# Self-attention of the second layer: the statistics of a coming batch from slot 4 to slot 7, its normalisation from slot 6 to slot 3 of the next batch

## The chip, the cores and the metric

The kernel runs on one core of one Trainium2 chip. Its engines run side by side and meet only at semaphores: PE (TensorE, matmuls), DVE (VectorE), ACT (ScalarE), POOL (GpSimd) and SP, which here only issues transfers. The metric is the device time of one execution in microseconds (us), lower is better, as the median of several runs.

## What is computed

The whole network is two gated layers of attention and feed-forward over x of shape (16, 256, 128). The change touches one of its eight phases, the causal self-attention of the second layer: 16 batches of 256 tokens with 128 channels, 16 heads of width 32. `_ln` at its head is the part that is moved.

```python
def _ln(x, g, b):
    m = jnp.mean(x, -1, keepdims=True)
    v = jnp.var(x, -1, keepdims=True)
    return (x - m) * jax.lax.rsqrt(v + 1e-05) * g + b

def _mha(x, y, ...):                       # here y is x
    xn = _ln(x, lnx_g, lnx_b)
    yn = _ln(y, lny_g, lny_b)
    q = jnp.einsum('bsc,hcd->bhsd', xn, wq)
    k = jnp.einsum('btc,hcd->bhtd', yn, wk)
    v = jnp.einsum('btc,hcd->bhtd', yn, wv)
    a = jax.nn.softmax(jnp.einsum('bhsd,bhtd->bhst', q, k) * D ** (-0.5), axis=-1)
    mask = (jnp.arange(t)[None, :] > jnp.arange(s)[:, None])
    a = a * mask
    o = jnp.einsum('bhst,bhtd->bhsd', a, v)
    x_out = x + o @ li1_w + li1_b
```

## The kernel before, in words

`network` lists eight phases, and between two phases all engines meet. The phase of the change is `SelfAttention(k, "d", 32, "after", ...)`, and in it `a.G` is 4. Phase "a", the first layer's self-attention, uses the same code with `a.G` 1 and other slots.

Each engine has a program of its own that walks the same slots, eight to a batch (`a.per`). A slot i of batch b is one unit, four heads by 128 queries by 256 keys. I number the slots of a batch 0 to 7. The order within an engine is fixed by this code; nothing is scheduled at run time.

In each slot PE runs a **window**: the scores of unit i (L441), then the transposed scores of unit i - 6 (`a.lag`) with their maxima subtracted (L466, L470). A window of slot i + 1 waits until the maxima and the exponentials of slot i are done, since both lie in the same PSUM banks (`wait(pe, s["maxed"], 2 * ...)` and `wait(pe, s["exped"], 2 * t)`). While DVE takes the maxima (L697, two per slot) and ACT the exponentials (L611, two per slot), PE runs `values` of unit i - 8 (L520, L525, L532) and then the slot's pieces.

The pieces and steps are in the table `SLOTS[4]`. Letters: T transposes the normalised input on PE (L547) and DVE scales it out of PSUM (L759, L760); Q, V are projections (PE L414, ACT L633, L634, L647); N transposes the split maxima (PE L576, then DVE L771); Y is the output projection (PE L414, DVE L778); U, R, M are steps on DVE alone (L729, L738, L745). The ones that matter here:

- slot 1: N of the second half of the batch in front, then V
- slot 3: R (a DVE transpose of 128x512, L738) and V
- slot 4: T of the next batch, M (a DVE multiplication of two SBUF tensors, L745), Q
- slot 5: N and Y; slot 7: `save_denominators` (L719) and Y

POOL masks each unit after its exponentials (L843), adds the two units of a pair in every odd slot (L851, 128x1024), splits the maxima of each half batch into bf16 parts (`split`, L822 to L830) at the head of slots 0 and 4, and adds a bias (L810) in slot 5.

The normalisation of batch b + 2 runs ahead of its use in three parts. `norm_stats` on DVE: two bn_stats (L166) and two bn_aggr (L171). `rstd` on POOL: an addition (L219) and a power (L221), behind a wait on `aggr`. `norm` on DVE: two tensor_scalar of 128x128 from SBUF to SBUF (L193), behind a wait on `rstd`. Before, DVE does the statistics at the end of slot 4 of batch b and `norm` at the end of slot 6; POOL does `rstd` at the end of slot 4. Piece T in slot 4 of batch b + 1 reads the result. Batches 0 and 1 are normalised ahead of the phase, so 14 batches go through this code.

SP loads x of batch b + 2 once `norm` of batch b has released the buffer (`wait(sp, s["wn"], b - 1)` in `sync_self`, called with b + 2). Behind it in SP's queue stand the load of the residual input, which waits for POOL's bias of an earlier batch, some transfers of blanks, and a store.

Of the kernel before, what the change touches and what calls it, by code (L numbers as in the profile page):

```python
# [6 lines left out]
B, S, C = 16, 256, 128  # L7
# [34 lines left out]
class Count:  # L42


    def __init__(self, sem):
        self.sem, self.n = sem, 0
# [194 lines left out]
class SelfAttention:  # L241
# [21 lines left out]
    def __init__(self, k, name, D, mask, src, base, dst, ctx, w):  # L263
        self.k, self.name, self.D, self.mask = k, name, D, mask
        self.src, self.base, self.dst, self.ctx, self.ctx_norm, self.w = src, base, dst, ctx, False, w
        self.scale = float(D) ** -0.5
        self.G = H * D // P
        self.units, self.lag = self.UNITS[self.G], {1: 8, 4: 6}[self.G]
        self.per = len(self.units)
        self.first_max = [0, 4]  # L270
        self.nv, self.ends, self.nq = (1, 1, 2) if self.G == 1 else (2, 2, 4)
        self.weights_ahead, self.loaded_ahead, self.ahead_over = [], None, 4
        each = dict(x_in=16, base_in=16, stored=16, stats=1, aggr=1, eps_in=1, rstd=1, wn=1, t_full=1, side=1, q_full=self.G,
                    q_ready=self.nq, v_full=self.nv, v_ready=self.nv, window=self.per, maxed=2 * self.per, exped=2 * self.per,
                    split=10, turned_max=2, max_ready=2, masked=8, pv_done=self.per, num_saved=QUADS if self.G == 4 else 1,
                    den_saved=1, rden=1, r_full=self.ends, ot=self.ends, y_full=self.ends, res=self.ends, biased=1)
        if self.G == 1:
            each.update(k_full=1, km_ready=QUADS + 1, ctx_in=16)
        if mask == "after":
            each.update(summed=QUADS)  # L280
        self.s = k.signals(each, B)
        sem, n = k.counts["window"]
        k.counts["window"] = sem, n + self.lag
# [81 lines left out]
def wait(eng, signal, n):  # L365

    if n > 0:
        eng.wait_ge(signal.sem, signal.base + n)
# [308 lines left out]
def vector_self(dve, a):  # L677
# [4 lines left out]
    def maxima(i):  # L682

        b, c, e = a.unit(i)
        t, part = i - a.lag, a.part(i)
        wait(dve, s["window"], i + 1)
        wait(dve, s["split"], 5 * (part - 1))
        for pair in range(2):
            if pair == 1 and a.is_unit(t):
                wait(dve, s["exped"], 2 * t + 1)  # L690
            out, banks = k.nmax[:, part % 2, 6 * e:6 * e + 6], a.score_banks(pair)
            if c == a.CROSS:
                last = dve.tensor_reduce(out[:, 2:6, 2 * pair:2 * pair + 2].rearrange("p c j -> p j c"),
                                         banks[:, :, 0:S].rearrange("p n (c t) -> p n c t", c=4), AX.X, ALU.max, negate=True)
            else:
                n = (e + 1) * P if a.mask == "before" else S
                last = dve.tensor_reduce(out[:, c % 2, 2 * pair:2 * pair + 2], banks[:, :, 0:n], AX.X, ALU.max, negate=True)  # L697
            last.then_inc(s["maxed"].sem, 1)

    def own_values(bank, b, blk):  # L700

        return dve.tensor_tensor(
            k.val[:, b % 2, blk].rearrange("p (r j c) -> p r j c", r=4, c=32),
            bank[:, blk * P:(blk + 1) * P].rearrange("p (r c) -> p r c", r=4).unsqueeze(2).to_broadcast([P, 4, 4, 32]),
            k.own_columns[:, :, :].unsqueeze(1).to_broadcast([P, 4, 4, 32]), ALU.mult)
# [8 lines left out]
    def save_denominators(b):  # L714

        wait(dve, s["pv_done"], a.per * (b + 1))
        wait(dve, s["rden"], b)
        if a.G == 4:
            dve.transpose(k.den[:, 0:S], k.turned[0][:, b % 2 * S:(b % 2 + 1) * S]).then_inc(s["den_saved"].sem, 1)  # L719
        else:  # L720
            dve.transpose(k.den, k.turned[0][:, :]).then_inc(s["den_saved"].sem, 1)
# [59 lines left out]
    for i in a.slots:  # L781
        if a.is_unit(i):
            maxima(i)
        n = i - a.lag - LATER
        if a.is_unit(n) and n % a.per == a.per - 1:
            save_denominators(n // a.per)
        for kind, m, b, which in a.pieces(i):
            piece(kind, m, b, which)
        for kind, m, b in a.steps(i):
            step(kind, m, b)  # L790
        for kind, m, b, which in a.pieces(i - 1):
            if kind == a.V and a.G == 1:
                own_values(a.bank(which), b, 1)
                cross_values(a.bank(which), b).then_inc(s["v_ready"].sem, 1)
        ahead = i // a.per + 2
        if 2 <= ahead < B and i % a.per == 4:
            norm_stats(Step(ahead))
        if 2 <= ahead < B and i % a.per == 6:
            norm(Step(ahead))


def gpsimd_self(pool, a):
    k, s, w = a.k, a.s, a.w

    rstd = attention_rstd(pool, a)

    def bias(b):
        wait(pool, s["base_in"], 16 * (b + 1))
        wait(pool, s["res"], a.ends * (b - 1))
        pool.tensor_tensor(k.base_sum[:, b % 2], k.base_in[:, b % 2], w["o_bias"].unsqueeze(1).to_broadcast([P, SB, C]), ALU.add)\  # L810
            .then_inc(s["biased"].sem, 1)

    def split(part):

        wait(pool, s["maxed"], 2 * a.part_end(part))
        wait(pool, s["turned_max"], part - 1)
        heads = 6 if a.G == 1 and part % 2 else 2
        order = lambda x: x.rearrange("p (e c) j -> p e j c", e=2)[:, :, :, 0:heads]
        parts = [k.nmax3[:, part % 2].rearrange("p e (j x) -> p e j x", x=32)[:, :, :, n:n + 3 * heads - 2:3] for n in range(3)]
        whole, rest = order(k.nmax[:, part % 2]), [order(k.nrest[:, n]) for n in range(2)]  # L820
        done = 5 * part
        pool.tensor_copy(parts[0], whole).then_inc(s["split"].sem, 1)  # L822
        wait(pool, s["split"], done + 1)
        pool.tensor_tensor(rest[0], whole, parts[0], ALU.subtract).then_inc(s["split"].sem, 1)
        wait(pool, s["split"], done + 2)
        pool.tensor_copy(parts[1], rest[0]).then_inc(s["split"].sem, 1)
        wait(pool, s["split"], done + 3)
        pool.tensor_tensor(rest[1], rest[0], parts[1], ALU.subtract).then_inc(s["split"].sem, 1)
        wait(pool, s["split"], done + 4)
        pool.tensor_copy(parts[2], rest[1]).then_inc(s["split"].sem, 1)  # L830

    def mask(t):

        b, c, e = a.unit(t)
        wait(pool, s["exped"], 2 * (t + 1))
        blk = a.keys_block(e)
        block = k.pt[:, t % TURNED, :, blk * P:(blk + 1) * P]
        if a.mask == "before":
            pool.affine_select(out=block, in_=block, compare_op=ALU.is_ge, fill=0.0, base=0, pattern=[[0, 4], [1, P]],  # L839
                               channel_multiplier=-1).then_inc(s["masked"].sem, 1)  # L840
        else:
            wait(pool, s["pv_done"], t - TURNED + 1)
            pool.affine_select(out=k.pm[:, t % TURNED], in_=block, compare_op=ALU.is_ge, fill=0.0, base=-1, pattern=[[0, 4], [-1, P]],  # L843
                               channel_multiplier=1).then_inc(s["masked"].sem, 1)

    def add(t):

        b, c, e = a.unit(t)
        wait(pool, s["exped"], 2 * (t + 1))
        wait(pool, s["pv_done"], t - 3)  # L850
        pool.tensor_tensor(k.both[:, c % 2], k.pt[:, (t - 1) % TURNED], k.pt[:, t % TURNED], ALU.add).then_inc(s["summed"].sem, 1)  # L851

    for i in a.slots:
        for part in range(2 * B):
            if a.part_end(part) == i:
                split(part)
        if a.is_unit(i - a.lag) and a.unit(i - a.lag)[1] < a.CROSS:
            mask(i - a.lag)
            if a.mask == "after" and (i - a.lag) % 2 == 1:
                add(i - a.lag)  # L860
        ahead = i // a.per + 2
        if 2 <= ahead < B and i % a.per == 4:
            rstd(Step(ahead))
        if i % a.per == 5 and 0 <= i // a.per - 1 < B:
            bias(i // a.per - 1)
# [1773 lines left out]
```

## Time and profile before

| | |
|---|---|
| time, median of 3 runs | 1555.57 us (1554.34 to 1556.86) |
| the profiled execution | 1551.26 us |
| its span in the profile | 1549.5 us |
| PE busy | 1322.5 us (85%) |
| DVE busy | 927.1 us (60%) |
| POOL busy | 769.1 us (50%) |
| ACT busy | 705.7 us (46%) |

The phase of the change runs from about 601 to 990 us of the span. A busy share over the whole span says little about one phase, so the rows below are taken from the order of time within one batch (window of slot 2 at 684.96 us to window of slot 2 at 708.74 us, a period of 23.78 us), from the summaries of waits, and from two places where engines met one another. In the views in order of time a row gives the start, the time from the first start to the last end of what is merged in it, engine, line, operation, what is written and read, and how many instructions; in brackets stands the idle time of the engine just before, and who ended it.

### The profile page before, as it was taken

The numbers are of one execution on the slowest core, as the hardware profiler recorded it, in microseconds if no ns is written. First come the engines' busy times: TensorE is split into PE (matmuls) and PEld (weight loads), VectorE is DVE, ScalarE is ACT, GpSimd is POOL, SyncE is SP. The second block draws the span as 40 slices with busy tenths as digits, with TensorE's granted clock in tenths as the row PEclk, the third lists the DMA queues.
The fourth block names the chain that finished last, engine by engine and source line by source line (L and its number), as shares of the span: only waits on it lengthen the run. The fifth ranks groups of instructions, "written<-read, shape, count | busy, mean of one in ns | idle before, by whom it ended". The sixth has DMA issues, their size and how long they took to land. (4 is left out here: it accounts for less than half of the span.)

```text
span 1549.5 us, 56395 instructions
## 1 busy us (share of the span) xinstructions
PE 1322.5 (85%) x22833; PEld 843.6 (54%) x22834; DVE 927.1 (60%) x2397; ACT 705.7 (46%) x1485; POOL 769.1 (50%) x1355
## 2 busy tenths in 40 slices
PE   3899999999985977999999999596999996893786
PEld 2555555555544653555555555364555554572676
DVE  3566666767654555776767766355467766584343
ACT  1455555455543434555565666242244442430443
POOL 3233333323330673877778787577222222576355
PEclk8899999999997888999999999798599999896899
DMA  3340000000000135334243342121011101232221
GB/s 80 78 131 18 21 17 21 14 21 13 14 9 22 55 102 156 105 93 132 68 133 103 98 126 68 42 82 56 20 32 36 34 24 47 86 103 73 68 77 49
DMA packets 145313, 97.92 MB, mean 63 GB/s; under 512 B 20533, under 2 KB 141964, under 8 KB 145068
## 3 DMA queue, kind: packets, MB, share of 16 engines
q1 hardware_dynamic: 142252, 88.06, 20.7%
q0 software_dynamic: 2816, 6.37, 1.1%
q8 instruction: 181, 2.97, 0.8%
q14 instruction: 64, 0.52, 0.1%
HBM read 40.31 MB, written 54.61 MB: 61 GB/s over the span
## 5 line engine op out<-in xcount | busy, mean ns | idle before, releaser
L611 ACT ACTIVATE space<-scores 128x512 f32<-128x512 f32 x576 | 314.0, 551 | 334.4 <-PE scores L470 221.1
L697 DVE TENSOR_REDUCE space<-scores 128x2 f32<-128x512 f32 (+1 forms) x512 | 306.7, 622 | 213.4 <-PE scores L470 147.5
L839 POOL TENSOR_SCALAR_AFFINE_SELECT space<-space 128x512 f32<-128x512 f32 x128 | 81.3, 635 | 274.0 <-ACT space L611 274.0
L441 PE MATMUL scores<-space 32*128 32x256 f32 (+1 forms) x2304 | 193.7, 404 | 22.8 <-DVE space L697 16.6
L470 PE MATMUL scores<-space 32*128 32x256 f32 (+1 forms) x2048 | 151.0, 357 | 1.5 <-issue 1.5
L851 POOL TENSOR_TENSOR space<-space 128x1024 f32<-128x1024 f32 x64 | 151.3, 2364 | 0.0
L441 PEld LDWEIGHTS scores<-space 32*128 32x128 f32 x2304 | 95.0, 188 | 88.4 <-DVE space L697 77.0
L843 POOL TENSOR_SCALAR_AFFINE_SELECT space<-space 128x512 f32<-128x512 f32 x128 | 88.0, 687 | 72.6 <-ACT space L611 72.5
L470 PEld LDWEIGHTS scores<-space 32*128 32x128 f32 x2048 | 84.5, 187 | 19.0 <-issue 2.1
L466 PE MATMUL scores<-space,selectors 32*128 32x256 bf16 (+1 forms) x1024 | 73.2, 255 | 6.5 <-issue 5.0
L166 DVE BATCH_NORM_STATS2 space<-space 128x6 f32<-128x128 f32 (+1 forms) x304 | 67.0, 273 | 18.2 <-DMA space<-xo 16.9
L1097 ACT ACTIVATE space<-scores 128x512 f32<-128x512 f32 x64 | 37.9, 597 | 82.4 <-PE scores L1006 77.7
L437 PE MATMUL scores<-above_parts,ident_parts 32*128 32x128 bf16 (+3 forms) x2048 | 42.8, 200 | 32.3 <-DVE space L697 20.4
L511 PE MATMUL turned<-space,ones_column 128*32 128x128 f32 (+1 forms) x1024 | 68.9, 341 | 0.3 <-POOL space L839 0.3
L437 PEld LDWEIGHTS scores<-above_parts,ident_parts 32*128 32x128 bf16 x2048 | 30.1, 94 | 70.6 <-DVE space L697 50.4
L1414 PE MATMUL turned<-w_a_li_w,space 128*128 128x128 f32 x512 | 67.3, 285 | 1.1
L1468 ACT ACTIVATE space<-scores,w_later_cols 128x512 f32<-128x512 f32 x96 | 59.4, 676 | 19.2 <-PE scores L1401 18.8
L1480 ACT ACTIVATE space<-space 128x128 f32<-128x128 f32 x72 | 29.7, 482 | 83.7 <-POOL space L1682 83.7
L514 PE MATMUL num<-space 128*32 128x128 f32 (+1 forms) x1024 | 65.5, 328 | 0.0
L1152 DVE TENSOR_REDUCE space<-scores 128x8 f32<-128x512 f32 x64 | 42.2, 692 | 38.2 <-PE scores L1006 33.2
L1414 PEld LDWEIGHTS turned<-w_a_li_w,space 128*128 128x128 f32 x512 | 61.6, 196 | 6.2 <-ACT space L1468 4.1
L1401 PE MATMUL scores<-space,w_a_li_w 128*128 128x512 f32 x128 | 62.9, 638 | 1.9 <-DVE space L1519 1.9
(324 smaller groups left out, 2877.6 us busy)
## 6 DMA issues: line engine op xcount, KB each, us to landing
by_expert<-blank SPq DMA_DIRECT2D x33, 1040.0 KB, 9.5
space<-by_expert SPq DMA_DIRECT2D x40, 130.0 KB
space<-in_x SPq DMA_DIRECT2D x32, 128.0 KB, 2.2
space<-xx SPq DMA_DIRECT2D x32, 128.0 KB, 2.5
xo<-space SPq DMA_DIRECT2D x32, 128.0 KB, 2.6
space<-xo SPq DMA_DIRECT2D x16, 256.0 KB
space<-xm SPq DMA_DIRECT2D x32, 128.0 KB, 2.2
w_w<-in_L_ffn_w SPq DMA_DIRECT2D x8, 256.0 KB
```

The lines of the kernel that those rows point to most:

```text
L166: last = dve.bn_stats(stats[:, blk], x[:, blk])
L437: pe.matmul(a.score_bank(j)[:, e * P + 32 * part:n], k.ident_parts[rows, part], k.above_parts[rows, part, 32 * part:P], start=(part == 0), ...
L441: last = pe.matmul(a.score_bank(j)[:, 0:n], q[rows, e * P:(e + 1) * P], keys[rows, 0:n], start=not cut, stop=True, skip_group_check=True)
L466: pe.matmul(a.score_bank(j)[:, S + lo:2 * S], k.selectors[rows, c % 2], a.maxima(t)[rows, lo:S], start=True, stop=False, skip_group_check= ...
L470: last = pe.matmul(a.score_bank(j)[:, S + lo:2 * S], keys[rows, blk * P:(blk + 1) * P], q[rows, lo:S], start=False, stop=True, skip_group_ ...
L511: pe.matmul(strip(k.turned[0], j)[:, lo:S], k.ones_column[:, c], pt[:, j, lo:S], start=first, stop=done, skip_group_check=True)
L611: act.activation(pt[:, 2 * pair:2 * pair + 2, lo:S], a.score_banks(pair)[:, :, S + lo:2 * S], ACT.Exp, bias=0.0, scale=1.0)\
L697: last = dve.tensor_reduce(out[:, c % 2, 2 * pair:2 * pair + 2], banks[:, :, 0:n], AX.X, ALU.max, negate=True)
L839: pool.affine_select(out=block, in_=block, compare_op=ALU.is_ge, fill=0.0, base=0, pattern=[[0, 4], [1, P]], channel_multiplier=-1).then_i ...
L843: pool.affine_select(out=k.pm[:, t % TURNED], in_=block, compare_op=ALU.is_ge, fill=0.0, base=-1, pattern=[[0, 4], [-1, P]], channel_multi ...
L851: pool.tensor_tensor(k.both[:, c % 2], k.pt[:, (t - 1) % TURNED], k.pt[:, t % TURNED], ALU.add).then_inc(s["summed"].sem, 1)
L1414: last = pe.matmul(k.turned[t.parity][:, blk * P:(blk + 1) * P], k.mh[:, t.parity, f, blk * P:(blk + 1) * P], w["w2"][:, f], start=(f == 0 ...
```

## The change

It gives the two slots names, `stats_slot` and `norm_slot`. For `a.G` 1 they keep their values (4 and 6). For `a.G` 4 the statistics go to slot 7, on DVE and with `rstd` on POOL, and `norm` goes to slot 3 of the next batch. The distance in batches is counted anew there, so that the same batches are normalised, one slot ahead of piece T that reads them.

```diff
+        self.stats_slot, self.norm_slot = {1: (4, 6), 4: (7, 3)}[self.G]
...
         ahead = i // a.per + 2
-        if 2 <= ahead < B and i % a.per == 4:
+        if 2 <= ahead < B and i % a.per == a.stats_slot:
             norm_stats(Step(ahead))
-        if 2 <= ahead < B and i % a.per == 6:
+        if a.norm_slot < a.stats_slot:
+            ahead = i // a.per + 1
+        if 2 <= ahead < B and i % a.per == a.norm_slot:
             norm(Step(ahead))
...
         ahead = i // a.per + 2
-        if 2 <= ahead < B and i % a.per == 4:
+        if 2 <= ahead < B and i % a.per == a.stats_slot:
             rstd(Step(ahead))
```

DVE, from the end of slot 2 to slot 6 of a batch in the middle of the phase, before. `space` is the name under which all SBUF work tiles go:

```order
L745 TENSOR_TENSOR space<-space 128x512
L697 TENSOR_REDUCE space<-scores 128x2 x2
L738 STREAM_TRANSPOSE space<-space 128x512
L697 TENSOR_REDUCE space<-scores 128x2 x2
L759 TENSOR_SCALAR space<-misc,w_later_cols 128x256
L760 TENSOR_SCALAR space<-misc,w_later_cols 128x256
L745 TENSOR_TENSOR space<-space 128x512
L166 BN_STATS space<-space 128x6 x2
L171 BN_AGGR space<-space 128x2 x2
L697 TENSOR_REDUCE space<-scores 128x2 x2
L771 COPY space<-turned 128x256
L778 TENSOR_TENSOR space<-misc,space 128x128
```

The same place now, with the line numbers of the changed file (one more for these lines):

```order
L746 TENSOR_TENSOR space<-space 128x512
L698 TENSOR_REDUCE space<-scores 128x2 x2
L739 STREAM_TRANSPOSE space<-space 128x512
L193 TENSOR_SCALAR space<-space 128x128 x2
L698 TENSOR_REDUCE space<-scores 128x2 x2
L760 TENSOR_SCALAR space<-misc,w_later_cols 128x256
L761 TENSOR_SCALAR space<-misc,w_later_cols 128x256
L746 TENSOR_TENSOR space<-space 128x512
L698 TENSOR_REDUCE space<-scores 128x2 x2
L772 COPY space<-turned 128x256
L779 TENSOR_TENSOR space<-misc,space 128x128
```

The four instructions of the statistics are gone from between M of slot 4 and the maxima of slot 5, and the two of `norm` stand between R of slot 3 and the maxima of slot 4.

POOL, from the mask of slot 4 over the bias to the split at the head of the next batch's slot 0, before:

```order
L843 AFFINE_SELECT space<-space 128x512
L219 TENSOR_TENSOR space<-space,eps 128x2
L221 TENSOR_TENSOR space<-space,minus_half 128x2
L843 AFFINE_SELECT space<-space 128x512
L851 TENSOR_TENSOR space<-space 128x1024
L810 TENSOR_TENSOR space<-space,w_a_li_b 128x256
L843 AFFINE_SELECT space<-space 128x512 x2
L851 TENSOR_TENSOR space<-space 128x1024
L822 CAST nmax<-space 128x8x2
```

The same place now, where the line numbers of POOL's program are higher by three:

```order
L846 AFFINE_SELECT space<-space 128x512 x2
L854 TENSOR_TENSOR space<-space 128x1024
L813 TENSOR_TENSOR space<-space,w_a_li_b 128x256
L846 AFFINE_SELECT space<-space 128x512 x2
L854 TENSOR_TENSOR space<-space 128x1024
L219 TENSOR_TENSOR space<-space,eps 128x2
L221 TENSOR_TENSOR space<-space,minus_half 128x2
L825 CAST nmax<-space 128x8x2
```

The two instructions of `rstd` have moved from between two masks to between the addition of slot 7 and the split of slot 0.

## Rows read from the trace of the kernel before

**Rows 1.** Busy time in the stretch 601 to 986 us; then PEclk, DMA share, GB/s.

```profile
601.00:986.00 385.00, 362.59 (x6810) 212.88 (x6810) 260.44 (x510) 226.29 (x470) 297.81 (x389) 1.00 0.35 96
```

**Rows 2.** Waits of PE, 660 to 935 us: total us, times, longest.

```profile
PE scores L441 <- DVE space L697: 4.6, 11, 0.4
```

**Rows 3.** DVE in order of time, slots 3 to 7 and the next slot 0.

```profile
690.26 0.70 DVE L738 STREAM_TRANSPOSE space<-space 128x512 f32<-128x512 f32 x1
691.86 1.32 DVE L697 TENSOR_REDUCE space<-scores 128x2 f32<-128x512 f32 x2 [0.91 <-PE scores L470]
693.64 0.54 DVE L759 TENSOR_SCALAR space<-misc,w_later_cols 128x256 f32<-128x256 f32 x1 [0.46 <-PE misc L547]
...
694.56 0.68 DVE L745 TENSOR_TENSOR space<-space 128x512 f32<-128x512 f32 x1
695.15 0.48 DVE L166 BATCH_NORM_STATS2 space<-space 128x6 f32<-128x128 f32 x2
...
695.83 1.25 DVE L697 TENSOR_REDUCE space<-scores 128x2 f32<-128x512 f32 x2
...
699.77 1.17 DVE L193 TENSOR_SCALAR space<-space 128x128 f32<-128x128 f32 x2
...
704.13 1.32 DVE L697 TENSOR_REDUCE space<-scores 128x2 f32<-128x512 f32 x2 [0.90 <-PE scores L470]
```

**Rows 4.** PE in order of time, same batch: windows of slots 5, 6, and N.

```profile
693.53 0.71 PE L441 MATMUL scores<-space 32*128 32x256 f32 x8
...
694.18 0.61 PE L470 MATMUL scores<-space 32*128 32x256 f32 x8
...
695.73 1.08 PE L414 MATMUL misc<-w_a_li_w,space 128*32 128x128 f32 x32
697.22 0.71 PE L441 MATMUL scores<-space 32*128 32x256 f32 x8 [0.42 <-DVE space L697]
...
707.53 0.29 PE L576 MATMUL turned<-identb,nmax 128*128 128x128 bf16 x2
```

**Rows 5.** POOL in order of time, same batch.

```profile
690.41 0.64 POOL L843 TENSOR_SCALAR_AFFINE_SELECT space<-space 128x512 f32<-128x512 f32 x1 [1.71 <-ACT space L611]
691.01 2.37 POOL L851 TENSOR_TENSOR space<-space 128x1024 f32<-128x1024 f32 x1
...
695.25 0.63 POOL L843 TENSOR_SCALAR_AFFINE_SELECT space<-space 128x512 f32<-128x512 f32 x1
696.00 0.19 POOL L219 TENSOR_TENSOR space<-space,eps 128x2 f32<-128x2 f32 x1
696.27 0.70 POOL L221 TENSOR_TENSOR space<-space,minus_half 128x2 f32<-128x2 f32 x1
...
697.81 2.37 POOL L851 TENSOR_TENSOR space<-space 128x1024 f32<-128x1024 f32 x1
700.13 0.73 POOL L810 TENSOR_TENSOR space<-space,w_a_li_b 128x256 f32<-128x256 f32 x1
...
703.27 2.37 POOL L851 TENSOR_TENSOR space<-space 128x1024 f32<-128x1024 f32 x1
705.58 0.23 POOL L822 CAST nmax<-space 128x16 bf16<-128x16 f32 x1
...
706.79 0.22 POOL L830 CAST nmax<-space 128x16 bf16<-128x16 f32 x1
```

**Rows 6.** POOL and PE in order of time, where PE waited for a split.

```profile
970.24 0.22 POOL L830 CAST nmax<-space 128x16 bf16<-128x16 f32 x1
...
970.61 0.27 PE L576 MATMUL turned<-identb,nmax 128*128 128x128 bf16 x2 [0.73 <-POOL nmax L830]
```

**Rows 7.** POOL and DVE in order of time, where M met an addition.

```profile
971.58 2.35 POOL L851 TENSOR_TENSOR space<-space 128x1024 f32<-128x1024 f32 x1
971.86 2.62 DVE L745 TENSOR_TENSOR space<-space 128x512 f32<-128x512 f32 x1
```

**Rows 8.** All of line 193: duration in ns, least, median, most.

```profile
L193 DVE TENSOR_SCALAR space<-space x96: 245/342/766, 18.9 to 1259.0; 128x128 f32<-128x128 f32 x96
```

## The prediction

> **What bounds the kernel now.** I read the page's list of busy times first, then the phase alone. From 601 to 986 us PE is busy for 362.6 of 385 us at a granted clock of 1.00, the upper level, 2.4 GHz [rows 1]. So PE sets the pace here, and an edit on DVE or POOL counts only by what it adds to or takes from PE's idle time. Next I read the summary of PE's waits: between 660 and 935 us it waits 11 times for DVE's maxima at the head of a window, 4.6 us in all, 0.42 us each [rows 2]. That is once a batch (a batch takes about 24 us), and the order of time shows where: the window of slot 6, at 697.22, starts 0.42 us after PE has run out of work [rows 4]. Its cause stands in DVE's rows: in slot 4 DVE runs T, M (0.68) and the statistics, and the maxima of slot 5 start at 695.83 with no idle time ahead of them, while the window they read, PE's L470, had ended at 694.18 + 0.61 = 694.79. They end at 697.08, and PE starts 0.14 later [rows 3, 4]. In the other slots the maxima have idle time in front: 0.91 us in slot 4, 0.90 in slot 0 [rows 3]. This is what the change is about: it takes DVE's work out of the slot that is too full.
>
> **Part 1, the statistics leave slot 4: a gain.** They take 695.83 - 695.15 = 0.68 us there [rows 3]. Without them the maxima of slot 5 start up to 0.68 earlier, which is more than the 0.42 that PE waits, and PE's own work (Y, ending at 695.73 + 1.08 = 696.81) is then the last thing in front of the window of slot 6. So the gain is the wait, 0.42 us, not the 0.68. M exists only from batch 2 and the statistics up to batch 13, so it comes 12 times: **-5.0 us**.
>
> **Part 2, the statistics arrive in slot 7: free.** DVE sits idle for 0.90 us before the maxima of slot 0 [rows 3], and 0.68 fits. They would stand beside POOL's addition of slot 7 (703.27 to 705.64) [rows 5]. Do the two block one another? In slot 4 the statistics run from 695.15 and POOL's mask from 695.25, and both take their usual time (0.48 for two, 0.63) [rows 3, 5]; the mask is not the addition, so this is the nearest row and not a proof. The statistics are done by about 704, ahead of 705.64, so POOL's rstd need not wait for them. If the addition did hold them up, they would end near 706 and the maxima of slot 0 would come over 1.5 us late: that is the bound, and I take nothing. The Trainium skill (SBUF — State Buffer, "Who interferes with whom") states that a DVE instruction with one SBUF input outside the two-port modes does not contend with GpSimd; by it this part costs nothing too.
>
> **Part 3, rstd stands before the split of slot 0: a cost.** Now the split starts at 705.58, directly behind the addition, and its last instruction ends at 706.79 + 0.22 = 707.01; PE's N starts at 707.53 [rows 4, 5]. So PE has 0.52 us in hand, less the time from POOL's end to PE's start, which is 970.61 - 970.46 = 0.15 where PE did wait for a split [rows 6]. rstd takes from 696.00 to 696.97, 0.97 us [rows 5]. POOL has no idle time between addition and split, so the whole of it goes into the split: end at 707.95 or so, N at 708.10 instead of 707.53. PE is in order, and V and the window of slot 2 stand behind N. Cost 0.57 us, 14 times: **+8.0 us**. In slot 4, where rstd stood, POOL had slack, and taking it away gives nothing.
>
> **Part 4, norm arrives in slot 3: the large term.** By busy time it would nearly fit: a tensor_scalar takes 0.25 to 0.34 us when nothing is in its way [rows 8], two of them 0.5 to 0.7, against 0.91 us of idle time. But the rows of slot 6 show something else. The two take 1.17 us there, 699.77 to 700.94. POOL's addition runs until 697.81 + 2.37 = 700.18, then its bias L810 from 700.13 to 700.86, and the pair ends 0.08 us after that [rows 3, 5]. I read it so: the first waits for the addition to end, runs, POOL's next instruction gets in, and the second waits for that one. All 12 pairs that have a bias beside them from 650 us on look like this one, 1.16 or 1.17 us. A DVE instruction held for a whole addition is in the trace as well: M at 971.86 takes 2.62 us instead of 0.68 and ends after the addition that began at 971.58 [rows 7].
>
> In slot 3, DVE's R ends at 690.26 + 0.70 = 690.96. POOL's mask runs until 691.01, and directly behind it comes the addition of 2.37 us [rows 3, 5]. So the place is the same as in slot 6, but what stands second on POOL is the long addition and not the bias of 0.73. The first norm goes in between mask and addition; the addition starts perhaps 0.13 late (the bias took 0.73 where a quarter of the addition's 2.37 is 0.59) and ends at 693.5; the second norm ends at 693.6. The maxima of slot 4 then start at 693.5 instead of 691.86, and end at 694.85. The window of slot 5 follows 0.14 later, at 694.99 instead of 693.53 [rows 4]: **1.45 us** lost on PE. T, which waits for norm, is ready at 693.6 and lies inside this wait. Does slot 5 stay free of its old wait? DVE has T (twice 0.54) and M (0.68) after 694.85 and is free near 696.5; PE's L470 of that window ends 1.26 after its start, at 696.25. The maxima end near 697.8, and PE has work until 694.99 + 3.28 = 698.27. So the gain of part 1 stays.
>
> How often: batch 1 has no R in front of norm, so there both instructions get by with the mask alone; batches 2 to 14 make 13. 13 x 1.45 = **+18.9 us**. Lower bound of the term: nothing, if the second norm gets in before the addition. Upper: if the first norm misses the gap, both stand behind the addition and among the short instructions of the split, some 0.3 us more each, +22.8.
>
> The Trainium skill (same page and section) says that for such a pair of ports the one that issues first holds it for the whole instruction and the other fully blocks, and that issue order decides. Rows 7 agree. It does not say who is first when the first norm ends: if it counts norm's second instruction as issued first, that is the rival below.
>
> **Part 5, norm leaves slot 6, and SP.** Slot 6 had idle time behind norm, so nothing is gained. SP's load of x for batch b + 2 waits for norm of batch b and so goes out about half a batch later. It still stands ahead of the load that waits for POOL's bias, so nothing behind it in the queue moves, and its reader, the statistics, has moved back three slots as well. Nothing.
>
> **Sum.** -5.0 + 8.0 + 18.9 = +21.9 us. The profiled execution took 1551.26 us, a span of 1549.5 with 1.8 around it; it would become 1573.2. Against the median of 1555.57, which is 4.3 higher for the same program, it is 1577.5, and I say 1577.
>
> **Rivals.**
> - *Both norms go in ahead of the addition.* DVE's second instruction wins the port. Then norm ends by 691.7 at the latest, before the maxima of slot 4 are due, and part 4 is nothing: -5.0 + 8.0 = +3.0, 1558.6, just within what can be told from no change. Against it: in slot 6 POOL's instruction got in between, 12 times of 12. For it: the first norm reaches the gap at 690.96 only, 0.05 us ahead of it, not 0.4 as in slot 6, and the order might differ. Chance 0.12.
> - *Nothing collides and POOL's delay is absorbed, faster.* As the last, and rstd finishes within the 0.37 us that N has in hand. The mechanism is the slot that is relieved: -5.0, 1550.6. It decides itself at the point where norm leaves less than 0.91 us behind R and the split less than 0.37 late. Against it: POOL's rows have no gap there. Chance 0.07.
> - *The collision, but no wait of N.* +18.9 - 5.0 = +13.9, 1569.5. Chance 0.12.
> - *The first norm misses the gap.* 0.3 x 13 = 3.9 more, 1581.5. Chance 0.10.
> - *The change does not do what it says.* The order of instructions shows that it does, so no chance is set aside. 0.04 is left for the unforeseen, on the slow side (statistics blocked in slot 7, say, over 20 us more).
>
> **How the numbers follow.** The forecast has 0.55: 1577, by itself 1573 to 1581. With the cases at 1569.5 and 1581.5 it comes to 0.77, and the bounds of the terms reach from 1567 to 1583; that is the range. It leaves out the first two rivals on purpose, which hold 0.19. A difference from 0.2% (3.1 us) upward can be told from no change. Faster: 0.07. Same: the first rival, 0.12. Slower: the rest, 0.81.
>
> **What would show it.** Right: the two norms of slot 3 take about 2.6 us together and end just after POOL's addition; the maxima of slot 4 lose their idle time; PE waits about 1.4 us for DVE at the window of slot 5 and no longer at that of slot 6; N waits about 0.5 us for the split. A batch takes some 1.6 us more. Wrong: norms of 0.7 us or less in slot 3 (part 4 falls), N without a wait (part 3), statistics of over 1 us in slot 7 (part 2), or a granted clock below 1.00 in this phase, which would move PE's own times.

## The result and the profile after

| | before | after |
|---|---|---|
| median of 20 runs of each | 1550.47 us (1537.98 to 1558.00) | 1566.07 us (1552.72 to 1571.13) |
| profiled execution | 1551.26 us | 1568.46 us |
| its span | 1549.5 us | 1566.7 us |

The ratio of after to before is 1.0085, with a 95% interval from 1.0056 to 1.0114: the change makes the kernel slower by 13.2 us, from 8.7 to 17.7 (the two medians as they stand differ by 15.6). The kernel before has a lower median here than in the three runs shown ahead of the prediction (1555.57).

The page of the changed kernel shows 21.7 us more busy time on DVE and 9.3 more on PE (before: 927.1 and 1322.5), though neither has more to do; a DVE instruction that is held up counts as busy, and the granted clock of the whole span is 0.932 instead of 0.936:

```profile
PE 1331.8 (85%) x22833; PEld 851.4 (54%) x22834; DVE 948.8 (61%) x2397; ACT 704.6 (45%) x1485; POOL 762.8 (49%) x1355
```

PE's waits from 660 to 935 us, against the one row of [rows 2]; the columns are the total, the times and the longest:

```profile
PE scores L442 <- DVE space L698: 8.5, 11, 0.8
PE turned L577 <- POOL nmax L833: 5.6, 11, 0.5
PE misc L548 <- DVE space L193: 4.5, 11, 0.4
```

One wait a batch has become three: for the maxima (0.77 instead of 0.42 us), for the split (0.51) and, in T, for norm (0.41). The order of time of one batch shows where each stands. DVE, slots 3 to 5 and 7, against [rows 3]:

```profile
691.90 0.70 DVE L739 STREAM_TRANSPOSE space<-space 128x512 f32<-128x512 f32 x1
692.53 2.62 DVE L193 TENSOR_SCALAR space<-space 128x128 f32<-128x128 f32 x2
695.07 1.27 DVE L698 TENSOR_REDUCE space<-scores 128x2 f32<-128x512 f32 x2
...
697.79 1.32 DVE L698 TENSOR_REDUCE space<-scores 128x2 f32<-128x512 f32 x2
...
705.62 0.48 DVE L166 BATCH_NORM_STATS2 space<-space 128x6 f32<-128x128 f32 x2
...
706.60 1.32 DVE L698 TENSOR_REDUCE space<-scores 128x2 f32<-128x512 f32 x2 [0.22 <-PE scores L471]
```

POOL, the same batch, against [rows 5]:

```profile
692.05 0.63 POOL L846 TENSOR_SCALAR_AFFINE_SELECT space<-space 128x512 f32<-128x512 f32 x1 [1.71 <-ACT space L612]
692.66 2.40 POOL L854 TENSOR_TENSOR space<-space 128x1024 f32<-128x1024 f32 x1
...
705.73 2.37 POOL L854 TENSOR_TENSOR space<-space 128x1024 f32<-128x1024 f32 x1
708.06 0.19 POOL L219 TENSOR_TENSOR space<-space,eps 128x2 f32<-128x2 f32 x1
708.33 0.70 POOL L221 TENSOR_TENSOR space<-space,minus_half 128x2 f32<-128x2 f32 x1
709.00 0.21 POOL L825 CAST nmax<-space 128x16 bf16<-128x16 f32 x1
...
710.20 0.22 POOL L833 CAST nmax<-space 128x16 bf16<-128x16 f32 x1
```

PE, the same batch, against [rows 4]: the windows of slots 4, 5, 6, T in front of the second, then the windows of slots 1 and 2 with N between them:

```profile
692.18 0.71 PE L442 MATMUL scores<-space 32*128 32x256 f32 x8
...
695.29 0.41 PE L548 MATMUL misc<-ident,space 128*128 128x128 f32 x2 [0.41 <-DVE space L193]
696.47 0.71 PE L442 MATMUL scores<-space 32*128 32x256 f32 x8 [0.77 <-DVE space L698]
...
699.68 0.71 PE L442 MATMUL scores<-space 32*128 32x256 f32 x8
...
708.02 0.71 PE L442 MATMUL scores<-space 32*128 32x256 f32 x8
...
710.57 0.27 PE L577 MATMUL turned<-identb,nmax 128*128 128x128 bf16 x2 [0.51 <-POOL nmax L833]
...
711.77 0.71 PE L442 MATMUL scores<-space 32*128 32x256 f32 x8
```

Norm's pair ends at 695.15, just behind POOL's addition, which ends at 695.06. The window of slot 5 comes 4.29 us after that of slot 4 (before: 693.53 - 690.54 = 2.99). The window of slot 6 follows after 3.21 instead of 3.69 us, with no wait. N waits 0.51 us, and slot 1 to 2 takes 3.75 instead of 3.19. A batch takes 25.17 instead of 23.78 us.

To compare whole phases I add up, over all batches, the distances from the start of one window to the start of the next, as PE's rows in order of time give them, by slot. All times are us. "Windows" is the sum, from the first window of the phase to its last (377.2 us before). Some expectations below count the phase from DVE's first maxima to its last Y, which is 404.5 us before.

| kernel | 0-1 | 1-2 | 2-3 | 3-4 | 4-5 | 5-6 | 6-7 | 7-0 | windows |
|---|---|---|---|---|---|---|---|---|---|
| before | 44.2 | 50.4 | 43.6 | 49.2 | 46.8 | 56.7 | 43.8 | 42.5 | 377.2 |
| before, second trace (e5) | 44.2 | 50.5 | 43.6 | 48.1 | 46.8 | 56.8 | 44.7 | 42.7 | 377.3 |
| after | 44.2 | 58.6 | 43.3 | 44.7 | 63.6 | 50.1 | 44.7 | 42.9 | 392.1 |
| after, second trace (e10) | 44.2 | 58.7 | 43.3 | 44.7 | 63.6 | 49.9 | 44.9 | 42.6 | 392.0 |
| e1 norm alone | 44.2 | 50.5 | 43.6 | 46.3 | 63.5 | 52.7 | 44.8 | 42.6 | 388.2 |
| e2 norm ahead of R | 44.2 | 58.6 | 43.3 | 44.8 | 46.8 | 49.9 | 43.9 | 42.5 | 374.1 |
| e3 rstd in slot 2 | 44.2 | 50.5 | 43.4 | 44.9 | 63.5 | 50.1 | 44.0 | 42.6 | 383.2 |
| e4 both | 44.2 | 50.5 | 43.3 | 45.0 | 46.8 | 49.9 | 43.9 | 42.5 | 366.2 |
| e6 x later | 44.2 | 50.6 | 43.3 | 47.0 | 46.8 | 56.7 | 44.6 | 42.8 | 376.0 |
| e7 blanks late | 44.2 | 50.5 | 43.3 | 44.6 | 46.8 | 56.8 | 44.9 | 42.5 | 373.6 |
| e8 short addition | 44.2 | 58.9 | 43.4 | 44.9 | 49.4 | 50.0 | 43.9 | 42.6 | 377.4 |
| e9 blanks at slot 0 | 44.2 | 50.5 | 43.3 | 51.7 | 50.9 | 56.9 | 43.8 | 42.5 | 383.9 |

From before to after four columns move: norm's collision in slot 4 to 5 **+16.8**, the wait of N in slot 1 to 2 **+8.2**, the relieved slot 5 to 6 **-6.6**, and slot 3 to 4 **-4.5**. The last has no term in the prediction. Together with small changes the phase gets 14.9 us longer, within the interval of the measured time. The small changes (+0.9) stand mostly in the slots 6 and 7 of batch 0, and the second trace of the kernel before has them too, so they are no effect of the change. The profiled executions differ by 17.2, the rest being outside this phase.

### The profile page after: what moved, and what is told of

It reads as the page before. It is cut to its first block and busy times, and to the rows that moved or that the text cites. A ratio compares the mean times of both kernels' runs of the same rounds, so it can differ in the third digit from the quotient of the medians.

```text
span 1566.7 us, 56395 instructions
## 1 busy us (share of the span) xinstructions
PE 1331.8 (85%) x22833; PEld 851.4 (54%) x22834; DVE 948.8 (61%) x2397; ACT 704.6 (45%) x1485; POOL 762.8 (49%) x1355
## 5 line engine op out<-in xcount | busy, mean ns | idle before, releaser
L471 PEld LDWEIGHTS scores<-space 32*128 32x128 f32 x2048 | 84.5, 187 | 17.2 <-issue 0.2
L1417 PE MATMUL turned<-w_a_li_w,space 128*128 128x128 f32 x512 | 71.7, 298 | 1.1
L438 PE MATMUL scores<-above_parts,ident_parts 32*128 32x128 bf16 (+3 forms) x2048 | 42.8, 200 | 32.1 <-DVE space L698 20.3
L1417 PEld LDWEIGHTS turned<-w_a_li_w,space 128*128 128x128 f32 x512 | 66.0, 208 | 6.1 <-ACT space L1471 4.1
L438 PEld LDWEIGHTS scores<-above_parts,ident_parts 32*128 32x128 bf16 x2048 | 30.0, 94 | 70.5 <-DVE space L698 50.1
```

What stands on the lines that cost most here:

```text
L438: pe.matmul(a.score_bank(j)[:, e * P + 32 * part:n], k.ident_parts[rows, part], k.above_parts[rows, part, 32 * part:P], start=(part == 0), ...
L471: last = pe.matmul(a.score_bank(j)[:, S + lo:2 * S], keys[rows, blk * P:(blk + 1) * P], q[rows, lo:S], start=False, stop=True, skip_group_ ...
L1417: last = pe.matmul(k.turned[t.parity][:, blk * P:(blk + 1) * P], k.mh[:, t.parity, f, blk * P:(blk + 1) * P], w["w2"][:, f], start=(f == 0 ...
```

## The experiments

**e1 and e3: one part at a time.** e1 keeps the statistics and rstd in slot 4 and moves only norm; e3 is the changed kernel with rstd on POOL behind the mask of slot 2.

```diff
# e1
-        self.stats_slot, self.norm_slot = {1: (4, 6), 4: (7, 3)}[self.G]
+        self.stats_slot, self.norm_slot = {1: (4, 6), 4: (4, 3)}[self.G]
# e3, gpsimd_self
-        if 2 <= ahead < B and i % a.per == a.stats_slot:
+        if a.G == 4:
+            ahead = i // a.per + 1
+        if 2 <= ahead < B and i % a.per == {1: 4, 4: 2}[a.G]:
             rstd(Step(ahead))
```

> Only norm is moved (to slot 3 of the next batch); the statistics and rstd stay in slot 4. Port theory (norm's second instruction waits for POOL's 128x1024 addition): the pair takes 2.6 us, the window of slot 5 comes 4.3 us after that of slot 4 instead of 2.99, PE's N in slot 1 does not wait for the split, slot 1 keeps its 3.19 us. Slot 5 to 6 stays near 3.4 (the statistics are still in slot 4). A batch takes 23.78 + 1.3 - 0.3 = 24.8 us, the phase some 13 us more than before. Rival (the loss of the change came from rstd's new place and not from norm): the pair takes under 1 us, the batch 23.8 us, the phase nothing more.

> The changed kernel, with rstd on POOL in slot 2 of the next batch, behind that slot's mask, instead of ahead of the split of slot 0. If the wait of N comes from rstd ahead of the split: N waits no longer, slot 1 to 2 falls from 3.75 to 3.19 us, the batch from 25.17 to 24.6, 8 us less in the phase. The pair of norms stays at 2.6 us. Rival (N waits for DVE or for the later bf16 parts, whatever stands in front of the split): 3.75 stays.

In e1 the pair takes as long as in the changed kernel. DVE of e1 in order of time:

```profile
720.08 2.61 DVE L193 TENSOR_SCALAR space<-space 128x128 f32<-128x128 f32 x2
...
722.61 1.28 DVE L698 TENSOR_REDUCE space<-scores 128x2 f32<-128x512 f32 x2
```

Slot 4 to 5 is 63.5 us, as after the change, and slot 1 to 2 is 50.5, as before it. So the loss in slot 4 to 5 comes from norm's place alone and needs neither the statistics nor rstd. The windows take 388.2 us, 10.9 more than before (expected 13): slot 3 to 4 is 2.9 us lower, which the expectation did not have. Slot 5 to 6 lies between the two kernels, 52.7 us (3.36 a batch), since the statistics are still in slot 4. One execution took 1553.63 us beside a median of 1542.40 before, whose 17 executions lie between 1540.13 and 1558.06; a single time says little here, the windows say more.

In e3 slot 1 to 2 falls from 58.6 to 50.5 us and nothing else moves by over 1 us: rstd ahead of the split is what N waits for. The phase is 9.0 us shorter than the changed kernel's (expected 8). Its one execution took 1552.32 us.

**e2: the same two instructions, 0.7 us earlier.** Norm goes ahead of R in slot 3. Nothing is taken away from DVE.

```diff
         for kind, m, b, which in a.pieces(i):
             piece(kind, m, b, which)
+        if a.G == 4 and 2 <= i // a.per + 1 < B and i % a.per == a.norm_slot:
+            norm(Step(i // a.per + 1))
         for kind, m, b in a.steps(i):
             step(kind, m, b)
...
-        if 2 <= ahead < B and i % a.per == a.norm_slot:
+        if a.G == 1 and 2 <= ahead < B and i % a.per == a.norm_slot:
             norm(Step(ahead))
```

> The changed kernel, with norm ahead of the transpose R in slot 3 instead of behind it. Port theory: norm's first instruction starts ahead of POOL's mask and the second goes in between mask and addition, as in batch 1 of the changed kernel, so the pair takes 0.9 us. R uses no shared port and is done at about the time at which the maxima of slot 4 are due. Slot 4 to 5 falls from 4.29 to 3.0 us, N still waits 0.5 us: a batch takes 25.17 - 1.3 = 23.9 us, 17 us less in the phase than the changed kernel. Rival (DVE simply has too much work in slot 3, maxima 1.3 + R 0.7 + norm 0.5 to 1.2 in 2.8 us): the order within the slot changes nothing, 25.2 us.

DVE and POOL of e2 in slot 3, in order of time:

```profile
716.79 0.91 DVE L193 TENSOR_SCALAR space<-space 128x128 f32<-128x128 f32 x2
716.94 0.68 POOL L848 TENSOR_SCALAR_AFFINE_SELECT space<-space 128x512 f32<-128x512 f32 x1 [1.71 <-ACT space L612]
...
717.59 2.37 POOL L856 TENSOR_TENSOR space<-space 128x1024 f32<-128x1024 f32 x1
717.62 0.70 DVE L739 STREAM_TRANSPOSE space<-space 128x512 f32<-128x512 f32 x1
```

The first norm is ahead of the mask, the second waits for the mask, as I read its 0.66 us, and gets in ahead of the addition, and R, a transpose, runs beside the addition at its usual 0.70. The pair takes 0.91 instead of 2.62 us. Slot 4 to 5 is back at 46.8 us, 16.8 less than in the changed kernel with the same work on DVE, so the rival of too much work in slot 3 falls. The phase is 18.0 us shorter than the changed kernel's (expected 17), and even 3 us shorter than before, because slots 3 to 4 and 5 to 6 keep their gains of 4.4 and 6.8 us against the 8.2 that N still costs. One execution: 1541.53 us.

**e8: the addition halved.** If the pair waits for the addition, it must follow its length.

```diff
-        pool.tensor_tensor(k.both[:, c % 2], k.pt[:, (t - 1) % TURNED], k.pt[:, t % TURNED], ALU.add)
+        pool.tensor_tensor(k.both[:, c % 2, 0:2], k.pt[:, (t - 1) % TURNED, 0:2], k.pt[:, t % TURNED, 0:2], ALU.add)
# tensor_self
-        k.both[:, c % 2, j],
+        k.both[:, c % 2, j % 2],
```

> The changed kernel, where POOL's addition covers two of the four heads (128x512 instead of 128x1024) and PE uses these two sums for all four: the denominators of the other two heads are left out. The addition falls from 2.37 to about 1.2 us. Port theory: norm's pair in slot 3 follows it one for one, from 2.62 to about 1.45 us, and slot 4 to 5 falls from 4.29 to 3.1 us. POOL also reaches rstd and the split 1.2 us earlier, so N waits no longer and slot 1 to 2 is 3.19 us. Rival (norm itself is slow beside any work of POOL): the pair stays above 2 us.

DVE and POOL of e8 in order of time:

```profile
711.57 1.52 DVE L193 TENSOR_SCALAR space<-space 128x128 f32<-128x128 f32 x2
711.70 1.31 POOL L854 TENSOR_TENSOR space<-space 128x512 f32<-128x512 f32 x1
...
713.02 1.27 DVE L698 TENSOR_REDUCE space<-scores 128x2 f32<-128x512 f32 x2
```

The addition shrinks by 1.09 us (2.40 to 1.31) and the pair by 1.10 (2.62 to 1.52). Slot 4 to 5 is 3.19 us a batch. One point was missed: slot 1 to 2 stays at 58.9 us in sum. Most batches have the expected 3.19 us there, but five have 3.7 to 6.7, and the one at 776 us shows PE in the middle of L533 without anything that it waits for. More on this below.

**e4: both mends together.** e2 and e3 in one kernel, with 12 executions.

> Both mends at once: statistics in slot 7, rstd in slot 2 of the next batch, norm in slot 3 ahead of R. Only the gain of the relieved slot 4 is left: the window of slot 6 comes 3.21 us after that of slot 5 (before: 3.69), 3.19 for slot 1, 3.0 for slot 4. A batch takes 23.3 us against 23.78 before, 12 times 0.48 = 5.8 us less in the phase than the kernel before, ratio 0.996. Rival (the relieved slot gains nothing, because the maxima and the exponentials of the next window take the place of the wait): ratio 1.000 and 3.69 or 3.6 us there.

DVE of e4, slots 3 to 5, in order of time:

```profile
710.64 0.92 DVE L193 TENSOR_SCALAR space<-space 128x128 f32<-128x128 f32 x2
...
712.25 1.32 DVE L698 TENSOR_REDUCE space<-scores 128x2 f32<-128x512 f32 x2
...
715.54 1.29 DVE L698 TENSOR_REDUCE space<-scores 128x2 f32<-128x512 f32 x2
```

The maxima of slot 5 still stand directly behind M, but PE no longer waits for them: slot 5 to 6 takes 3.20 us. **e4 is faster than the kernel before**, by 0.6%: 1534.75 us against 1542.40 on the same chip, ratio 0.9936 with an interval from 0.9903 to 0.9970 (expected 0.996). It was not timed beside the changed kernel, whose ratio to the kernel before is 1.0085. Its windows take 366.2 us, 11.0 less than before, where I had expected 5.8. The relieved slot gives 6.8 of it. The rest is again the column of slot 3 to 4, 4.2 us, for which the expectation had nothing.

**e5, e10, e6, e7, e9: what goes on in slot 3 to 4.** In the kernel before PE stands still there in three batches. PE in order of time, within a window, with nothing waited for ("issue"):

```profile
662.95 0.63 PE L470 MATMUL scores<-space 32*128 32x256 f32 x5
664.48 0.70 PE L470 MATMUL scores<-space 32*128 32x256 f32 x3 [0.91 <-issue]
```

Is it chance? e5 and e10 are the two kernels once more, with no edit.

> The kernel before, unchanged, a second trace of it. In its first trace PE stood still three times for 1.3 to 1.6 us in the window of slot 3 (4.43, 4.14 and 4.43 us from there to slot 4 instead of 2.84) with nothing that it waited for, 4.5 us in all; the changed kernel shows 0.1 us of it. If that belongs to the kernel before (its transfers of blanks and PE's instructions coming late behind them), the same three stand here again and its phase is again 404.5 us. If it is chance, they are elsewhere or gone, and the phase is near 400.

> The changed kernel, unchanged, a second trace of it. If its parts are fixed by the order of the work, the sums over the batches agree with its first trace within 0.3 us: slot 1 to 2 58.6, slot 3 to 4 44.7, slot 4 to 5 63.6, slot 5 to 6 50.1 us, all windows 392.2 us. If PE's stalls come and go by chance, slot 3 to 4 moves by 1 us or more.

The places are not chance, the size is in part. The second trace of the kernel before has the extra time in the same three batches (1.0, 1.0 and 1.3 us instead of 1.6, 1.3 and 1.6), and the changed kernel has 0.1 us of it in each of two traces, as expected of e10. Some 10 us before each stall SP has sent out blanks. SP's queue before, then after:

```profile
652.20 1.89 SPq L400 DMA_DIRECT2D by_expert<-blank  x2
654.13 1.44 SPq L392 DMA_DIRECT2D xo<-space  x1
655.67 1.24 SPq L378 DMA_DIRECT2D space<-xx  x1
```

```profile
652.97 1.57 SPq L401 DMA_DIRECT2D by_expert<-blank  x2
655.38 1.03 SPq L393 DMA_DIRECT2D xo<-space  x1
670.04 0.37 SPq L379 DMA_DIRECT2D space<-xx  x1
```

Before, the load of x follows the blanks at once and makes the burst longer; after, it goes out 14.7 us behind the store. And the blanks start a little sooner in PE's program: 1.38 us after the window of slot 7 before (652.20 against 650.81), 0.89 after the change (652.97 against 652.08), since POOL's bias, which no longer stands behind rstd, is done 0.5 us sooner and the load of the residual input ahead of the blanks waits for it. e7 takes the blanks away, e6 takes the load of x out of the burst, e9 starts the burst later.

```diff
# e7, sync_self: blanks of this phase only behind its last store
-        if b < a.ahead_over:
+        if b < a.ahead_over and a.G == 1:
...
+    if a.G == 4:
+        for dst, src in a.weights_ahead:
+            sp.dma_start(dst, src).then_inc(a.loaded_ahead, 16)
# e6, load_x in sync_self
+        if a.G == 4:
+            wait(sp, s["window"], a.per * (b - 3) + 4)
# e9, ahead of the blanks of each batch
+            if a.G == 4:
+                wait(sp, s["window"], a.per * b + 1)
```

> The kernel before, with all transfers of blanks of this phase issued at its end instead of two in each batch (the phases behind it get slower; only this phase is looked at). If PE's instructions come late because they stand behind the blanks: no stall is left, the phase is some 4.5 us shorter than the kernel before's, near 400. If the stalls have to do with PE's code alone, they stay at 1.3 to 1.6 us, three times.

> The kernel before, with SP's load of x held back until the window of slot 3 of the next batch, which is where it goes out in the changed kernel. In the kernel before it is issued directly behind the blanks and the store and lengthens their burst. If this is why the three stalls are gone after the change: slot 3 to 4 is 2.84 us in every batch, and the phase is some 4 us shorter than the kernel before's, near 400. If not, the three stalls stay and the phase is 404.

> The kernel before, with SP holding the blanks of each batch back until PE has done the window of slot 0, some 2 to 3 us later than they go out now; nothing else changes. If PE's stalls in slot 3 are a matter of where in PE's program the burst of blanks begins: they move to later slots or change in size (the sum over the batches of slot 3 to 4, 48.1 us in the second trace of the kernel before, falls to about 45, and another slot's sum rises). If only the length of the burst counts, they stay in slot 3 with the 3.4 us that they take now.

Without blanks in the phase slot 3 to 4 falls to 44.6 us, 2.83 in every full batch: the stalls need the blanks. With x out of the burst it is 47.0, a third of the effect against the second trace of the kernel before, a half against the first; its expectation of no stall at all failed. With the burst 3.4 us later in PE's program the stalls grow, 51.7 in slot 3 to 4 and 50.9 instead of 46.8 in slot 4 to 5, and the phase takes 6.7 us more than before. That slot 3 to 4 would fall to 45 was expected of e9 and failed; that another slot's sum rises came true. SP and PE's waits of e9 from 610 to 985 us:

```profile
653.38 1.27 SPq L402 DMA_DIRECT2D by_expert<-blank  x2
```

```profile
PE scores L468 <- issue: 4.3, 6, 1.0
PE scores L443 <- issue: 2.5, 2, 1.9
```

So the start and the length of the burst in relation to PE's program decide, and the change moved both the right way without meaning to. The other runs tell the two apart. Where x is late and the blanks go out 1.38 us after the window of slot 7, as before the change, slot 3 to 4 is 47.0 us (e6) and 46.3 (e1). Where x is late and the blanks go out 0.9 to 1.2 us after it, it is 44.7 to 45.0 (the changed kernel, e2, e3, e4).

What PE lacks in these moments is its own instructions, and the kept traces show it transfer by transfer. The queue q8 brings 16 KB at a time, in the kernel before 55 times from 600 to 980 us, one transfer for every 256 of PE's instructions. Over all traces PE stands still 19 times for more than 0.3 us between two matmuls with nothing waited for, up to the last window of the phase: three times each before and in e5, once in e1, twice in e6, four times in e8, six in e9. I counted PE's instructions from the first window of the phase, weight loads and those of its sequencer included. Each time PE has issued 256 n + 79, 80 or 81 of them, where n is the number of q8 transfers begun since, and it goes on 1.24 to 1.60 us after the last of these has ended. Ahead of the stall at 664.48 that transfer ran from 661.83 to 662.89. The one before it had ended at 652.96, and from 652.97 to 661.82 there was none, while SP's queue q1 filled the DMA engines. Packets, MB and share of the 16 engines, from 652.97 to 661.82, then from 661.8 to 662.9 us:

```profile
q1 hardware_dynamic: 2701, 2.43, 98.9%
```

```profile
q8 instruction: 1, 0.02, 6.0%
```

For the three transfers at which the kernel before stands still, this is the time in us from their end to the same instruction of PE:

| transfer | before | after | e7, no blanks |
|---|---|---|---|
| 9th, batch 3 | 1.60 | 1.93 | 4.15 |
| 16th, batch 5 | 1.35 | 2.27 | 3.79 |
| 23rd, batch 7 | 1.26 | 2.40 | 6.28 |

So the blanks make PE's instructions late, and after the change they come just in time. That the transfer starts late because it stands behind the blanks' packets on the same DMA engines is my reading of it; no row shows it wait.

This also tells e8 from e4. In e8 the blanks go out 1.3 us sooner in PE's program than in e4. The 26th transfer begins at 774.00, inside the burst of 768.7 to 777.8, and PE stands still in slot 1. In e4 it begins at 768.04, half a microsecond ahead of the burst, and is there 5.0 us before PE needs it. Two stalls cost more than their own time: after the 1.69 us in e8 at 922 us and the 1.95 in e9 at 885 the granted clock is 0.50, the lower level of 1.2 GHz, for some 3.5 us, and in e8 the eight matmuls of V take 1.85 us there instead of 1.06.

## Why the prediction was right or wrong

The direction held, and so did the mechanism of parts 1 to 4; the time did not: 1566.07 us is 0.9 below the range, and 11 below the forecast. The step that failed is part 5, which set the effect on SP's queue to nothing; with it failed the base on which the sum was laid. The miss of the range is small: the base, part 5, part 4 and part 1 are each off by more than 0.9 us. The lower end of the range, 1567, comes from no sum that the prediction shows. Point by point:

- **Part 4, norm beside POOL's addition: right, a little too large.** The pair takes 2.61 or 2.62 us in all 13 batches from 2 on, and 0.91 in batch 1, as the prediction has it. e2 and e8 show that it is the addition. A batch loses 1.30 and not 1.45 us. Two terms were too big: the first norm holds the addition up by 0.03 (it takes 2.40 us) and not by 0.13, a figure I had taken from the bias, and the maxima behind it take 1.27 and not 1.32. 16.8 instead of 18.9.
- **Part 3, rstd ahead of the split: right.** 8.2 us for a forecast of 8.0, 0.56 in most batches; e3 takes it away alone. Its last sentence, that taking rstd out of slot 4 gives nothing, was wrong: the bias behind it is done 0.5 us sooner, and so are the blanks (see part 5).
- **Part 1, the relieved slot 4: right, too small.** The wait of 0.42 us had hidden another 0.06, because the window that need not wait starts ahead of the end of Y in the rows. That is 0.48 for 12 batches. And batches 0 and 1, which I had left out because they have no M, gain 0.65 and 0.33: 3.08 us before and 2.75 after in batch 1. -6.6 instead of -5.0.
- **Part 2, the statistics in slot 7: right.** They take 0.48 for two beside the addition, and the maxima of slot 0 keep 0.22 us of idle time.
- **Part 5, "nothing": wrong.** This is the step that failed. I asked who behind the load of x in SP's queue gets later, and nobody does. I did not ask what the load of x and the bias do to the burst of blanks, and did not give the three stalls on PE, which stood in the trace of before, a place in the sum. They go with the change: -4.5 us against the first trace, -3.4 against the second. PE had stood there without its instructions, whose transfers came late through the burst of blanks; after the change the burst is shorter and ends earlier in PE's program.
- **The base.** The sum was laid on 1555.57, the median of three runs; the median of twenty is 1550.47. That is 5.1 of the 11 us. Outside this phase the time moves by more than that from run to run: the spans of the two traces of the kernel before are 1549.5 and 1539.3, with windows of 377.2 and 377.3 us in this phase. The granted clock goes with it: 0.81 in the first trace and 0.87 in the second from 985 to 1100 us, 0.90 and 1.00 from 1100 to 1200.

By terms: 16.82 + 8.25 - 6.64 - 4.46 = 13.97, with 0.95 of small changes 14.92, where the prediction had 21.9. None of the rivals took place.

## What to carry to other kernels

Before moving a DVE instruction that GpSimd's instructions can hold up (here tensor_scalar and tensor_tensor from SBUF to SBUF), look at which instructions stand on GpSimd at that time: of two such instructions in a row, the second waited here for the whole of whatever GpSimd had next, so what counts is the length of that one, and a place 0.7 us earlier can be worth 1.3 us a batch. When an engine's step is moved ahead of another step, add its time to everything behind it until the next idle time of that engine. And before calling a shift in a DMA queue free, look for bursts in it and for stalls elsewhere without a releaser: they may go or come with it.

## What the runs showed of the hardware

- DVE's norms and GpSimd's instructions take turns: between two norms ready back to back, POOL's waiting instruction came in every time, 12 or 13 times in a trace: a bias of 0.73, an addition of 2.40 or one of 1.31 us. A DVE transpose (0.70 us), bn_stats (0.48 for two) and maxima, which read PSUM (0.69 each), take their usual time beside the same addition.
- PE can stand still for 0.4 to 2 us without waiting for any semaphore while 2.4 to 2.5 MB of other data are under way, because the next 256 of its instructions (16 KB) have not come: all 19 such stalls end 1.24 to 1.60 us after the end of a transfer on the instruction queue. They come in the same batches in two traces of one program, and move with the start of the burst.
- In this phase two traces of one kernel agree within 0.15 us in 377, in part by luck: in the kernel before slot 3 to 4 moved by 1.1 us and slot 6 to 7 by 0.9 the other way. The columns that carry the argument, 4 to 5 and 5 to 6, moved by 0.2 us at most, while whole executions differ by 10 us and more. A difference of a few us in one phase is read much better from the windows' distances than from the time of the kernel.
